# Fused graph layer on one core: query weights ahead of the bias columns, M in one piece, a new order in the second graph's step and the last full step

## The reference

```python
h = relu(layernorm(x))                                  # layer 0
q, k, v = h @ Wq.T + bq, h @ Wk.T + bk, h @ Wv.T + bv
a = adj * exp(q @ k.T);  a = a / a.sum(axis=2)
x1 = x + a @ v
h1 = relu(layernorm(x1))                                # layer 1
A = adj + eye;  dn = A.sum(-1) ** -0.5
out = x1 + (dn[:, None] * A * dn[None, :]) @ (h1 @ W + b)
```

## Time and profile before

| what | value |
|---|---|
| median of 3 runs | 1633.62 us |
| the profiled execution | 1633.5 us, span 1631.7 us |
| PE busy / PE weight loads | 1622.8 us (99%) / 1544.9 us (95%) |
| DVE, ACT, POOL busy | 1346.4 us (83%), 1075.2 us (66%), 802.1 us (49%) |
| mean granted TensorE clock | 0.999 |
| chain that ended last | PE 95%, DVE 3%, SP's queue 1%, issue 1% |

### The profile page before, as it was taken

How to read it: one execution, slowest core, us unless ns; L and a number is a source line. 1 busy time by engine, 2 the same in 40 slices (tenths; PEclk the granted TensorE clock), 3 DMA queues, 4 the chain that set the end, 5 groups by cost and what they waited for, 6 DMA issues and landing times.

```text
span 1631.7 us, 37843 instructions
## 1 busy us (share of the span) xinstructions
PE 1622.8 (99%) x12061; PEld 1544.9 (95%) x12061; DVE 1346.4 (83%) x3370; ACT 1075.2 (66%) x2450; POOL 802.1 (49%) x970
## 2 busy tenths in 40 slices
PE   9999999999999999999999999999999999999999
PEld 7899999999999999999999999999999999999998
DVE  6888888888888888888888888888888888888886
ACT  5676666666766766766766667667667667666663
POOL 3545544544554455455445445544554554454452
PEclk9999999999999999999999999999999999999999
DMA  5455455455455464464554554554644545545531
GB/s 184 115 128 153 124 124 151 116 134 150 109 144 133 109 159 126 117 156 122 124 151 117 133 150 109 143 133 109 158 125 118 154 124 124 151 118 133 146 89 49
DMA packets 494559, 212.66 MB, mean 130 GB/s; under 512 B 402512, under 2 KB 427344, under 8 KB 494544
## 3 DMA queue, kind: packets, MB, share of 16 engines
q1 hardware_dynamic: 492624, 210.89, 50.2%
q10 hardware_dynamic: 1920, 1.58, 0.3%
HBM read 146.28 MB, written 66.13 MB: 130 GB/s over the span
## 4 chain that ended last, share of the span: by engine, by line
PE 95%; DVE 3%; SPq 1%; issue 1%; ACT 0%; DMA 0%; POOL 0%; POOLq 0%; DVEq 0%; ACTq 0%
PE ps L982 32%; PE ps L984 31%; PE ps L985 31%; SPq L180 1%; DMA adj_blocks<-in_adj_dram 0%; DVE ht_lo L779 0%; DVE wt_lo L664 0%; DVE unused_a L941 0%; DVE g_lo L675 0%; DVE m_lo L626 0%; DVE w_lo L669 0%; DVE z_lo L762 0%; DVE wt L651 0%; SPq L210 0%; DVE late L795 0%
## 5 line engine op out<-in xcount | busy, mean ns | idle before, releaser
L454 ACT ACTIVATE g_hi<-ps,u_col 128x256 fp32r<-128x256 f32 x256 | 106.0, 465 | 310.0 <-PE ps L985 310.0
L309 POOL TENSOR_TENSOR xb<-xb,bv_row 128x512 f32<-128x512 f32 x128 | 163.5, 1299 | 275.1 <-DVE late L768 271.9
L982 PE MATMUL ps<-ht_hi,m_hi 128*128 128x256 f32 x1024 | 287.0, 280 | 2.0 <-DVE ht_lo L779 1.8
L984 PE MATMUL ps<-ht_lo,m_hi 128*128 128x256 f32 x1024 | 286.6, 280 | 0.0
L985 PE MATMUL ps<-ht_hi,m_lo 128*128 128x256 f32 x1024 | 286.3, 280 | 0.0
L982 PE MATMUL ps<-w_hi,z_hi 128*128 128x512 f32 (+1 forms) x516 | 203.1, 394 | 0.7 <-DVE z_lo L762 0.7
L985 PE MATMUL ps<-w_hi,z_lo 128*128 128x512 f32 (+1 forms) x516 | 202.8, 393 | 0.0
L984 PE MATMUL ps<-w_lo,z_hi 128*128 128x512 f32 (+1 forms) x516 | 202.5, 392 | 0.0
L982 PEld LDWEIGHTS ps<-ht_hi,m_hi 128*128 128x128 f32 x1024 | 193.2, 189 | 2.4 <-issue 2.0
L985 PEld LDWEIGHTS ps<-ht_hi,m_lo 128*128 128x128 f32 x1024 | 193.2, 189 | 0.0
L984 PEld LDWEIGHTS ps<-ht_lo,m_hi 128*128 128x128 f32 x1024 | 193.2, 189 | 0.0
(11 more groups left out here) (165 smaller groups left out, 5507.0 us busy)
## 6 DMA issues: line engine op xcount, KB each, us to landing
x_in<-in_x_dram SPq DMA_DIRECT2D x64, 512.0 KB, 5.1
xb<-in_x_dram SPq DMA_DIRECT2D x64, 512.0 KB, 4.5
out_dram<-late SPq DMA_DIRECT2D x127, 256.0 KB, 2.1
h_scratch<-h SPq DMA_DIRECT2D x62, 512.0 KB, 2.8
h_blocks<-h_scratch SPq DMA_DIRECT2D x248, 128.0 KB, 3.9
adj_in<-in_adj_dram SPq DMA_DIRECT2D x64, 256.0 KB, 3.0
adj_blocks<-in_adj_dram SPq DMA_DIRECT2D x256, 64.0 KB, 2.5
dn_row<-dn_scratch SPq DMA_DIRECT2D x64, 128.0 KB, 2.9
```

Source lines behind the costliest of these rows:

```text
L309: last = pool.tensor_tensor(xb[:, t, :], xb[:, t, :], bv_row[:], ALU.add)
L454: last = act.activation(g_hi[:, m, :], ps[:, G + j, m % 2 * N:m % 2 * N + N], ACT.Identity, bias=u_col[:, m:m + 1])
L982: pe.matmul(dst, a_hi[:, c, cols], b_hi[:, c, :], start=(first and c == 0), stop=False, skip_group_check=not first)
L984: pe.matmul(dst, a_hi[:, c, cols], b_lo[:, c, :], start=False, stop=False, skip_group_check=not first)
```

## The change

Four parts:

1. ScalarE's queue issues the four query weight parts first and the bias columns behind them. The warm-up has 8 matmuls in place of 17, and all of M is made ahead of the transposes (before, its last quarter stood behind them).
2. Step 2. TensorE's V6 waits for the first half of the low block sums only, V7 for the second. GpSimd makes the second half behind `ln_1_ready`, and the block sums of the next graph behind `ht_lo_ready[1]`. ScalarE keeps V1 ahead of the `h1` passes and V5 between them, and does `z_high` ahead of the x sums and squares. VectorE moves `value_u2` and half of `w_low` forward, and `ht_low` directly behind the transposes, ahead of the row sums and of `x_shift`.
3. Step 64. TensorE's order is G, V, S, N, O, R (both halves), in place of G, V, N, S, R(0), O, R(1). `z_high` and `z_low` go behind the high and low parts of p. O(1) goes to bank 0 (`O_LAST`).
4. Step 65. The 14 filling matmuls go, with their wait for `y_ready`. VectorE makes all of graph 63's result here: `result(0)` between the two `h1_low` (before in step 64), `result(1)` behind the second (before between them).

```diff
@@ -115,7 +115,7 @@
         HT = (2, 4)
-        O = (6, 2)
+        O, O_LAST = (6, 2), (6, 0)
         VA, VB, VC, VD = 4, 5, 6, 7
@@ -361,6 +361,7 @@
                 if prev and not older:
+                    pool.wait_ge(ln_1_ready, this - 1)
                     ht_sums_low_half(this, 1)
@@ -393,6 +394,8 @@
                     pool.wait_ge(v_done[V3], this)
+                    if prev and not older:
+                        pool.wait_ge(ht_lo_ready[1], this + 1)
                     ht_sums(this + 1)
@@ -401,12 +404,12 @@
         def _(act):
+            for o in range(DC):
+                act.dma_start(wq_in[:, o, :], wq[o * P:(o + 1) * P, :]).then_inc(wqk_loaded[o], 16)
             act.dma_start(bq_col[:], bq.rearrange("(c p) -> p c", p=P),
...
                           allow_slow_non_contiguous=True).then_inc(columns_loaded, 16)
-            for o in range(DC):
-                act.dma_start(wq_in[:, o, :], wq[o * P:(o + 1) * P, :]).then_inc(wqk_loaded[o], 16)
             act.dma_start(bv_row[:], bv.partition_broadcast(P)).then_inc(bias_rows_loaded, 16)
@@ -515,6 +518,8 @@
+                    if main and not older:
+                        keep_p1(this)
                     for t in range(NT):
@@ -522,14 +527,13 @@
                         if main and not older and t == 0:
-                            keep_p1(this)
+                            keep_p5(this)
                 if main:
...
                     if prev and not older:
-                        keep_p5(this)
                         g_high(0, this)
@@ -538,10 +542,12 @@
                         layer_norm_x(this, prev, older)
-                    elif second:
+                    elif second and older:
                         x_sums(this + 2)
...
                         z_high(this - 1)
+                        x_sums(this + 2)
+                        x_squares(this + 2)
                     act.wait_ge(v12_ready, this)
@@ -559,13 +565,13 @@
                     wt_high()
-                if prev and older:
+                if prev and older and (ahead or not main):
                     z_high(this - 1)
...
                     act.activation(v_hi[:, 1, :, 0:HD], v[:, 1, :, 0:HD], ACT.Copy).then_inc(v_hi_ready[2], 1)
-                    if second and prev:
+                    if second and prev and older:
                         x_squares(this + 2)
@@ -575,6 +581,8 @@
                         act.activation(p_hi[:, t, :], p[:, t, :], ACT.Copy).then_inc(p_hi_ready[t], 1)
+                if main and not ahead:
+                    z_high(this - 1)
                 if main and ahead:
@@ -788,11 +796,12 @@
-            def keep_x1(t, graph):
+            def keep_x1(t, graph, banks=O):
+                bank = banks[t]
                 dve.wait_ge(o_done[t], graph)
-                dve.reciprocal(rinv[:, t:t + 1], ps[:, O[t], HD:HD + 1]).then_inc(rinv_ready[t], 1)
+                dve.reciprocal(rinv[:, t:t + 1], ps[:, bank, HD:HD + 1]).then_inc(rinv_ready[t], 1)
                 dve.wait_ge(rinv_ready[t], graph)
-                dve.scalar_tensor_tensor(halves(x1[:, t, :]), ps[:, O[t]:O[t] + 2, 0:HD], rinv[:, t:t + 1],
+                dve.scalar_tensor_tensor(halves(x1[:, t, :]), ps[:, bank:bank + 2, 0:HD], rinv[:, t:t + 1],
                                          halves(xb[:, t, :]), ALU.mult, ALU.add).then_inc(x1_ready[t], 1)
@@ -824,15 +833,17 @@
                     dve.wait_ge(dn_ready, this - 1)
-                    keep_x1(0, this - 1)
+                    keep_x1(0, this - 1, O_LAST)
                     last_variance(0, this - 1)
-                    keep_x1(1, this - 1)
+                    keep_x1(1, this - 1, O_LAST)
                     last_scale(0, this - 1)
...
                     h1_low(0, this - 1)
+                    dve.wait_ge(stored, (this - 3) * (16 * NT))
+                    result(0, this - 2, d)
+                    h1_low(1, this - 1)
                     result(1, this - 2, d)
-                    h1_low(1, this - 1)
                     dve.wait_ge(y_ready[0], this - 2)
@@ -866,10 +877,11 @@
                         g_low(0, this)
+                    if not older:
+                        value_u2(this)
+                        w_low(slice(0, 2))
                     h1_low(0, this - 1)
                     add_bias(0, this - 1)
-                    if not older:
-                        value_u2(this)
                     h1_low(1, this - 1)
@@ -885,7 +897,6 @@
                     value_low(this)
-                    w_low(slice(0, 2))
                     z_low(this - 1)
@@ -929,7 +940,9 @@
                         transpose_h(this)
-                        x_shift(this + 2)
+                        ht_low(this + 1, None)
+                if main and not ahead:
+                    z_low(this - 1)
                 if main and not prev:
@@ -944,8 +957,10 @@
                     dve.tensor_tensor(sd[:], s_sum[:], dn[:], ALU.mult).then_inc(sd_ready, 1)
-                if main and ahead and prev:
+                if main and ahead and prev and older:
                     ht_low(this + 1, None)
+                if main and prev and not older:
+                    x_shift(this + 2)
                 if ahead and not main:
@@ -954,12 +969,11 @@
                     x_mean(this + 2)
-                if prev and main:
+                if prev and main and ahead:
                     if older:
...
                     result(0, this - 1, d)
-                    if ahead:
-                        result(1, this - 1, d)
+                    result(1, this - 1, d)
                 if prev and not main:
@@ -989,7 +1003,7 @@
                 pe.wait_ge(consts_ready, 1)
-                for k in range(17):
+                for k in range(8):
                     pe.matmul(ps[:, WARM_BANK, 0:P], ones[:], ones[:], start=True, stop=True)
@@ -1056,7 +1070,7 @@
                 value(V1, VA, ht_rows(0), upper, B11, HD + 2)
-                pe.wait_ge(ht_sum_lo_ready, 2 * this)
+                pe.wait_ge(ht_sum_lo_ready, 2 * this - 1)
                 weights_ready(3)
@@ -1069,6 +1083,7 @@
                 pe.wait_ge(v_u2_ready, this)
+                pe.wait_ge(ht_sum_lo_ready, 2 * this)
                 weights_ready(7)
@@ -1091,11 +1106,27 @@
+            def neighbours(this):
+
+                pe.wait_ge(hat_lo_ready, this - 1)
+                pe.wait_ge(h1_lo_ready[1], this - 1)
+                for m in range(DC):
+                    cols = slice(m * P, (m + 1) * P)
+                    last = product(ps[:, Z + m // 2, m % 2 * N:m % 2 * N + N], NT,
+                                   (h1_hi, h1_lo), cols, (hat_hi, hat_lo))
+                    if m % 2:
+                        last.then_inc(z_done[m // 2], 1)
+
+            def scores(this):
+
+                pe.wait_ge(g_lo_ready[1], this)
+                for t in range(NT):
+                    cols = slice(t * P, (t + 1) * P)
+                    product(ps[:, G + t, 0:N], DC,
+                            (g_hi, g_lo), cols, (ht_hi, ht_lo)).then_inc(s_done[t], 1)
+
             def last_graph(graph):
-                pe.wait_ge(y_ready[0], graph - 1)
-                for k in range(14):
-                    pe.matmul(ps[:, O1, 0:N], p_hi[:, 0, 0:P], p_hi[:, 1, :], start=True, stop=True)
                 pe.wait_ge(hat_lo_ready, graph)
@@ -1136,31 +1167,19 @@
                     values(this, prev, older)
-                if main and prev:
-
-                    pe.wait_ge(hat_lo_ready, this - 1)
-                    pe.wait_ge(h1_lo_ready[1], this - 1)
-                    for m in range(DC):
-                        cols = slice(m * P, (m + 1) * P)
-                        last = product(ps[:, Z + m // 2, m % 2 * N:m % 2 * N + N], NT,
-                                       (h1_hi, h1_lo), cols, (hat_hi, hat_lo))
-                        if m % 2:
-                            last.then_inc(z_done[m // 2], 1)
+                if main and prev and ahead:
+                    neighbours(this)
                 if main:
-
-                    pe.wait_ge(g_lo_ready[1], this)
-                    for t in range(NT):
-                        cols = slice(t * P, (t + 1) * P)
-                        product(ps[:, G + t, 0:N], DC,
-                                (g_hi, g_lo), cols, (ht_hi, ht_lo)).then_inc(s_done[t], 1)
+                    scores(this)
+                if main and not ahead:
+                    neighbours(this)
                 if ahead and not main:
                     warm_up()
-                    m_product(range(DC - 1))
+                    m_product(range(DC))
                     pe.wait_ge(ident_ready, 1)
...
                     transpose_wv(range(2))
-                    m_product(range(DC - 1, DC))
                     pe.wait_ge(wvt_kept[0], 2)
@@ -1174,10 +1193,9 @@
                         pe.matmul(ps[:, Z, 0:N], m_hi[:, 0, 0:P], m_hi[:, 0, 0:N], start=True, stop=True)
-                if main and prev:
```

(7 more changed lines are left out.)

## The result

The changed kernel takes 1639.89 us (median of 6 executions, 1638.66 to 1641.45) against 1633.66 before; the ratio is 1.0038 with a 95% interval of 1.0028 to 1.0048. It is slower, by 6.2 us. The forecast was 1635.8 with a range to 1639.2: the sign of the sum was right, its size was not, and the time lies 0.7 outside. The profiled execution is 1640.99 us (span 1639.2), 7.5 over that of before, and 1.1 over its own median.

A forecast was written before the change was run, and what follows sets the result against it. The prediction took PE, busy 99% of 1631.7 us, as the bound, with no recurring wait in the loop. Its terms, 2.3 + 1.0 - 1.0 + 1.2 - 1.2 = +2.3 on 1633.5, gave 1635.8 us, range 1630.4 to 1639.2.

The forecast's parts named there:

- What bounds the kernel: Whole kernel: PE busy 99%, no wait recurs in the loop, so only the start, steps 2 and 3 and the end can gain.
- The columns' landing: Start: bias columns, queued behind four query weight parts, land at 10.9 us, bounds 9.5 and 11.8.
- the term of +2.3: Start: late columns delay VectorE's layer norm, so the `ht` copy and G(1) come 2.3 us later.
- B: Rival, start: the columns land by 8.6, so VectorE isn't late and TensorE's idles don't come; 1632.6 us, chance 0.20.
- D: Rival, start and V2: columns at 11.8, longer low clock, TensorE possibly last at G(1); 1639.4 us, chance 0.17.
- The clock at the start: Start: TensorE idles around the value weights' transposes and then runs at low clock; +1.0 us, between 0 and 3.2.
- Steps 2 and 3: G(3) starts 3.4 us earlier, but V2(3) waits 3.9 for `v_p` and gains only 1.0, bounds 1.5 and 0.2.
- the two readings of the sums: Step 3, GpSimd's block sums: shortening to 3.2 us gives -1.5; keeping 4.1 beside VectorE's row sums gives -0.6.
- The clock behind V2(3): Step 3: TensorE's idle of 3.9 us at V2 is followed by low clock; +1.2 us, between 0 and 2.6.
- Rival C: Steps 2 and 3: V2(3) doesn't wait, so step 2 gives its full 5.0 us; 1630.7 us, chance 0.18.
- The end: Steps 64 and 65: earlier z gains 1.7 us, `result(1)` costs 0.3 and O(1) 0.1 to 0.2; sum -1.2.
- the first `rinv`: End, last graph's layer 1: can start at 1611.5 instead of 1613.17, 1.7 us earlier.

The follow-up runs named there:

- run 7: Changed kernel with the bias columns loaded as 128 packets of 16 bytes each instead of 512 of 4 bytes (output not the layer's): 1636.47 us, ratio 1.0016.
- run 1: Changed kernel with the two bias columns ahead of the query weights on ScalarE's queue again; short warm-up and M in one piece stay: 1637.66 us, ratio 1.0024.
- run 2: Kernel before with the new start alone (query weights ahead of the columns, 8 warm-up matmuls, M in one piece): 1639.93 us, ratio 1.0041.
- run 4: Changed kernel with VectorE's wait for the columns and its eight products moved behind the layer norm's small instructions: 1637.59 us, ratio 1.0023.
- run 11: Changed kernel, new start kept, with 27 filling matmuls ahead of the wait at V2(3): 1639.74 us, ratio 1.0033.
- run 3: Changed kernel with the whole start of before (columns first, warm-up of 17, M's last quarter behind the transposes): 1633.31 us, ratio 0.9998.
- run 10: Changed kernel with the old start, step 3 taken out of the loop, and 27 filling matmuls ahead of the wait at V2(3): 1631.54 us, ratio 0.9987.
- run 12: As run 11, with 34 more filling matmuls of 128 columns between M's end and the wait for `h`: 1638.93 us, ratio 1.0030.
- run 8: Changed kernel with the old start, step 3 taken out of the loop and ScalarE's copy of V1 there ahead of its four `h1` passes: 1633.73 us, ratio 0.9998.
- run 9: As run 8, with `value_u2` directly behind `nb_1` and ScalarE's copy of V5 between the `h1` passes in step 3: 1631.46 us, ratio 0.9986.
- run 6: Kernel before with the changed steps 64 and 65 alone: 1633.35 us, ratio 0.9997.
- run 5: Kernel before with the changed step 2 alone, old start and old end: 1634.72 us, ratio 1.0006.

## Why the prediction failed where it did

**What bounds the kernel** was right: no wait recurs in the loop, and only the start, steps 2 and 3 and the end moved.

**The columns' landing is the step that failed.** The working had the last query part at 8.4, gave the columns 1.3 us each behind it, 11.0, took 10.9 and bounded them by 11.8. The last part landed at 9.7 and the columns at 12.6 and 15.2: of the 4.3 that they are late, 1.3 is the query weights' and 3.0 the columns' own. The 1.3 a column was the distance of their landings in the old order, when SP's queue had just begun and paused for a part of it. Behind the query weights each of their 512 packets of 4 bytes takes turns on its DMA engine with a 2 KB packet of SP's queue and costs 0.081 us, 2.6 a column; run 7 shows it by cutting the packets to a quarter, and the packet counts under run 7 show the turns. The upper bound was none: it assumed that the same six transfers end at the same time in any order. The Trainium skill (DMA: Bandwidth & Descriptors, Queues, rings and completion order) says that each DMA engine serves its queues in turn, packet by packet; by that rule a queue of tiny packets beside one of large packets is paid in packets and not in bytes, which is what run 7 measured, and the trace agrees with 360 small packets for 357 large ones. The rest of that paragraph held: 5.4 for the products, `neg_mean` and the norm behind them, 0.4 of slack (0.57 forecast), VectorE without a pause from the `ht` copy on. So the term of +2.3 measured +6.9. Of the rivals, B priced columns that land earlier, and only D ones that land later, by 0.9.

**The clock at the start**, +1.0, was 0.06 in the profiled execution (and 0.1 to 0.2 in those of runs 1, 2 and 7), 1.3 in run 4 and 1.9 in run 11. The mechanism of rival D (TensorE last at G(1) behind bias products at half clock) is real and comes in some executions; the 3.2 of its upper bound was not reached. D's number, 1639.4, is the nearest of the four, but that is luck, for its way there was another: D asked for late columns by 0.9 and two episodes; the late columns alone were worth 4.6 more than forecast, and in the profiled execution the clock at the start was worth nearly nothing.

**Steps 2 and 3**: G(3) 3.34 earlier relative to the start (3.4 forecast); V2(3) 1.52 earlier (1.0 forecast, bound 1.5), waiting 3.29 (3.9), released by `v_p` as said. `hat_low` ended 7.87 behind the first sum's start, in place of 8.66. Of the two readings of the sums in the earlier trace rows, the second was the nearer: they took 3.25 from 79.33 to 82.58, though they ran beside VectorE's row sums. The prediction had looked at the wrong VectorE instruction. Before, the third sum of GpSimd ran beside `ht_low`, which has two SBUF inputs, and both were long; now `ht_low` is done before the sums start. Before, then now:

```profile
74.24 1.81 DVE L779 TENSOR_TENSOR ht_lo<-ht,ht_hi 128x512 fp32r<-128x512 f32 x2
74.26 1.24 POOL L320 TENSOR_TENSOR ht_sum<-ht_sum,ht 128x256 f32<-128x256 f32 x1
```

```profile
77.91 1.29 DVE L787 TENSOR_TENSOR ht_lo<-ht,ht_hi 128x512 fp32r<-128x512 f32 x2
81.03 0.74 POOL L320 TENSOR_TENSOR ht_sum<-ht_sum,ht 128x256 f32<-128x256 f32 x1
```

The third and fourth sums took 1.24 and 1.06 before and 0.74 each now, 0.8 less, which is the whole gain of `hat_low`; the first two, beside the row sums, took 0.86 and 0.91 before and 0.85 and 0.91 now, and VectorE's second row sum 0.95 in both. The clock behind V2(3) cost 2.7 in the profiled execution against 1.2 forecast and a bound of 2.6; over executions 0.2 (run 3's profile) to 2.7, about 1.8 in the median by runs 3 and 10. Rival C fell: with the changed step 2, V2(3) waits 3.3 wherever its wait is not filled (runs 10 to 12) and ScalarE's order is not changed (runs 8 and 9), and 8 shows that taking that wait away only uncovers the next.

**The end**: -1.2 forecast, -0.6 measured. `result(1)` ahead of the low part of z fits the 0.3 that the working gave it: R waits 1.07 for `z_low` where it waited 0.70. What failed is the first `rinv`, 0.7 later than said: the row sums were taken at their old length of 1.1, and moved to where GpSimd's `hat_low` starts, 1.53 for the first. The Trainium skill (SBUF — State Buffer, Who interferes with whom) says that a VectorE instruction with two SBUF inputs and a GpSimd instruction that reads SBUF hold a shared port pair exclusively and the later one blocks; the rows agree in kind, 0.05 us of lead for GpSimd and 0.85 us of delay for VectorE, and run 6 has the same 1.53 again; a block to the very end of `hat_low` would be 1.25. The prediction used the rule in step 2 and not here. Whether a start of the row sums ahead of `hat_low` gives the 0.7 back was not tried.

**Sum.** 6.95 + 1.16 - 0.62 = +7.5 in the profiled execution, against 3.3 + 0.2 - 1.2 = +2.3. 3.6 of the 5.2 are at the start (the late landing, +4.6, less the clock that didn't count, -0.9); 1.0 in step 3, 0.6 at the end.

## What to carry to other kernels

Price a small strided load by its packets, and by what the other queues move at the same time; here an early column costs 1.3 us and a late one 2.6, and what hangs on it may be a chain far longer than its 2 KB suggest. Before a gain is booked, follow the chain of the next wait with its slack (V2(3) had 0.25 us), and of the one behind it: here three waits in a row (V2, V7, N) stood for the same lateness of VectorE, and moving one copy alone gave nothing. An idle of 3.3 us on TensorE was followed by half clock in five of six profiled executions, at a price of up to 2.7 us; filling it with idle matmuls (run 10) or shortening all of its causes together (run 9) were the two versions that beat both kernels, by 0.13% and 0.14%, both with the old start.

## What the runs showed that I had not expected

- The same idle of 3.3 us at V2(3) was followed by a granted clock of 1.00 in one execution (run 3) and by 0.58 and 0.70 over a stretch of 5 us in others (the changed kernel, run 5); G(4) came 16.5 to 19.0 us behind V2(3). Executions of one kernel with such an idle scatter over 2 to 4 us, where before stays within 1.3 (1633.21 to 1634.55 in 27 executions). What decides it in one execution is not shown.
- In the kernel before, G(3) at half clock (1.6 us longer) and G(3) at full clock with a wait of 1.17 at V2(3) (run 6, which has the same steps 2 and 3) give the same G(4), 102.65 and 102.55.
- M at a clock that fell behind an idle of 2.87 took 15.7 us in place of 14.3 (run 1); there the short warm-up saved nothing, since M waited for its load in any case.
